# A convolution and mixture-of-experts layer in fp32: low halves of the expert weights made by negated copies and adding DMAs, buffers laid out anew, no float copy of the top indices

## The reference, cut to what matters

```
u  = x @ W_in + b_in; uc = short_conv(u)         # 3 taps, 768 channels
x0, x1, v = split(uc);  v = v * x1
v  = causal_fft_conv(v, filter) + filter_bias    # long convolution over 512 tokens
x  = layernorm(x + (v * x0) @ W_out + b_out)
probs = softmax(x @ gate.T);  top_w, top_idx = top_k(probs, 4)      # 16 experts
y  = sum over the 4 experts of  top_w/sum(top_w) * (silu(x@w1.T) * (x@w3.T)) @ w2.T
x  = layernorm(x + y + shared_expert(x))
```

## Time and profile before

| | |
|---|---|
| three runs | 797.89, 795.56, 797.14 us; median 797.14 |
| profiled execution, first to last instruction (its span) | 696.8 us |
| TensorE | busy 561.5 us (81%), mean granted clock 0.931 |
| VectorE | busy 543.4 us (78%) |
| ScalarE | busy 400.4 us (57%) |
| GpSimd | busy 439.5 us (63%) |
| DMA | 127.69 MB, mean 183 GB/s |

### The profile page before, as it was taken

How to read it: one execution, slowest core, us unless ns; L and a number is a source line. 1 busy time by engine, 2 the same in 40 slices (tenths; PEclk the granted TensorE clock), 3 DMA queues, 4 the chain that set the end, 5 groups by cost and what they waited for, 6 DMA issues and landing times.

```text
span 696.8 us, 13551 instructions
## 1 busy us (share of the span) xinstructions
PE 561.5 (81%) x3356; PEld 491.9 (71%) x3357; DVE 543.4 (78%) x1492; ACT 400.4 (57%) x968; POOL 439.5 (63%) x417
## 2 busy tenths in 40 slices
PE   1789798999999999997268799999899996777600
PEld 0568686888888887876156799899899886767500
DVE  5438699999999999998976566566666568989877
ACT  0635264776767566762134677676677775666632
POOL 2060325486868676767907677777776668777882
PEclk9979899999999999999759999999999999999965
DMA  8339811342333333247843567765655569998674
GB/s 305 108 104 316 287 56 35 107 137 100 115 117 127 105 129 102 97 158 227 263 129 120 185 204 222 233 207 183 187 181 175 166 238 377 279 299 265 239 272 173
DMA packets 77116, 127.69 MB, mean 183 GB/s; under 512 B 10870, under 2 KB 57527, under 8 KB 76474
## 3 DMA queue, kind: packets, MB, share of 16 engines
q1 hardware_dynamic: 45548, 69.34, 32.3%
q0 software_dynamic: 22448, 49.17, 20.1%
q10 hardware_dynamic: 9086, 8.80, 3.7%
HBM read 81.00 MB, written 54.72 MB: 195 GB/s over the span
## 4 chain that ended last, share of the span: by engine, by line
DVE 37%; PE 36%; issue 15%; ACT 4%; POOL 4%; DMA 3%; DVEq 1%; SPq 0%; POOLq 0%; ACTq 0%
PE bank L856 6%; PE bank L857 5%; PE bank L858 5%; PE bank L895 3%; PE bank L687 3%; DVE prodA L1208 2%; POOL token_parts L648 2%; DVE i8f L1265 2%; DVE prodB L1209 2%; PE bank L796 2%; DVE x1c L1129 2%; PE bank L706 2%; PE bank L887 2%; DVE stats L1148 2%; DMA token_parts<-late,wd 2%
## 5 line engine op out<-in xcount | busy, mean ns | idle before, releaser
L648 POOL DMA_INDIRECT token_parts<-late,wd x160 | 156.6, 979 | 67.2 <-issue 40.8
L635 POOL DMA_INDIRECT expert_rows<-row,slot x128 | 131.4, 1026 | 95.5 <-DVE dest L1345 38.8
L856 PE MATMUL bank<-w_hi,xtT_hi 128*128 x320 | 94.0, 294 | 22.2 <-issue 12.6
L1391 DVE TENSOR_TENSOR ta<-bank,tsl 128x128 f32<-128x128 f32 x160 | 46.3, 289 | 66.7 <-ACT tsl L1049 65.0
L1067 ACT ACTIVATE late<-bank,wd 128x256 f32<-128x256 f32 x160 | 76.4, 478 | 37.5 <-DMA token_parts<-late,wd 31.8
L857 PE MATMUL bank<-w_lo,xtT_hi 128*128 x320 | 91.8, 287 | 0.0
L858 PE MATMUL bank<-w_hi,xtT_lo 128*128 x320 | 91.7, 287 | 0.0
L856 PEld LDWEIGHTS bank<-w_hi,xtT_hi 128*128 128x128 f32 x320 | 62.4, 195 | 26.7 <-issue 26.7
L1404 DVE TENSOR_TENSOR xtT_lo<-bank,xtT_hi 128x256 fp32r<-128x256 f32 x160 | 67.6, 423 | 1.1 <-ACT xtT_hi L1060 0.6
L1049 ACT ACTIVATE tsl<-bank 128x128 f32<-128x128 f32 x160 | 44.1, 276 | 39.3 <-PE bank L858 37.5
L1060 ACT CAST xtT_hi<-bank 128x256 fp32r<-128x256 f32 x160 | 61.8, 387 | 6.1 <-PE bank L895 5.7
(11 more groups left out here) (176 smaller groups left out, 1513.5 us busy)
## 6 DMA issues: line engine op xcount, KB each, us to landing
xt<-expert_rows SPq DMA_DIRECT2D x160, 129.0 KB
row<-token_parts SPq DMA_DIRECT2D x12, 640.0 KB, 5.2
more_parts<-token_parts SPq DMA_DIRECT2D x12, 640.0 KB, 8.7
late<-token_parts SPq DMA_DIRECT2D x8, 640.0 KB, 7.8
expert_rows<-in_c_pad SPq DMA_DIRECT2D x2, 2064.0 KB, 14.0
expert_rows<-in_c_pad SPq DMA_DIRECT2D x32, 129.0 KB
xT_hi<-in_xT POOLq DMA_DIRECT2D x8, 512.0 KB, 4.3
xT<-in_xT SPq DMA_DIRECT2D x8, 512.0 KB, 3.9
```

What stands on the lines that cost most here:

```text
L635: pool.indirect_dma_start(out=rows_d, out_offset=bass.IndirectOffsetOnAxis(ap=slot[q][:, n:n + 1], axis=0), in_=row[:, n // TOPK, n % TOPK ...
L648: pool.indirect_dma_start(out=parts_d, out_offset=bass.IndirectOffsetOnAxis(ap=wd[:, v, 1:2].bitcast(U32), axis=0), in_=ty[v % 4], in_offs ...
L856: te_.matmul(ps, x_hi, w_hi, start=first, stop=False)
```

## The change

1. The loads of w2_in and w13 by SP, `low_bits` and `low_bits2` are gone. Instead ACT writes the negated high half into the low half's buffer in body(7) (8192 and 4096 elements on each partition), and POOL adds the weights to it by five DMAs with an adding write: four for w13 after the eighth of the 16 scatters of body(6), one for w2 after the sixteenth. So they come ahead of POOL's bias addition of body(7).
2. PE waits for these five DMAs ahead of the second stage, in place of the subtractions.
3. DVE compares `eidx` with the uint32 indices themselves; `i8f` and one count of `dve_top` go.
4. The buffers are in another order in memory. SP's loads of `xt` wait for the forward transform of batch 7 in place of its inverse.

The diff, without the rest of the new order of buffers (all same sizes; `late` is split in ty_all, s2, ob0 and late_parts, and w2_in is gone):

```diff
-        ARG_N, TOP_N, SLOT_N, TAB_N = 7, 2 * TT + 5, 5, 13
+        ARG_N, TOP_N, SLOT_N, TAB_N = 7, 2 * TT + 4, 5, 13
...
-        def low_bits(eng, ops, n):
-            eng.wait_ge(ld_moe, 32)
-            eng.wait_ge(ld_w13[n], 16)
-            at = slice(n * PART, (n + 1) * PART)
-            ops.tensor_tensor(out=w13_lo[:, at], in0=w13_lo[:, at].bitcast(F32), in1=w13_hi[:, at].bitcast(F32),
-                              op=ALU.subtract).then_inc(lo_made, 1)
...
 # SP, body(7)
-                    sp.wait_ge(dve_conv, 2 * VC * B)
-                    sp.wait_ge(pool_conv, 2 * DC * B)
-                    sp.wait_ge(pe_u, UC * B)
-                    sp.dma_start(w2_in[:, :].rearrange("p (e d) -> p e d", e=E),
-                                 io["w2"].rearrange("e h d -> h e d")).then_inc(ld_w2, 16)
-                    sp.wait_ge(pe_fwd, 2 * NF * B)
-                    sp.wait_ge(dve_Y, 2 * NF * B)
-                    k = E // NPART
-                    for n in range(NPART):
-                        sp.dma_start(w13_lo[:, n * PART:(n + 1) * PART].bitcast(F32)...
 # SP, ahead of the second stage
-            sp.wait_ge(dve_y, DC * B)
+            sp.wait_ge(pe_fwd, 2 * NF * B)
...
 # POOL
-                if isinstance(i, int) and i == B - 1:
-                    for n in range(NPART - 1):
-                        low_bits(pool, nc.gpsimd, n)
...
                         for n in range(TT * TOPK):
+                            if isinstance(i, int) and i == B - 2 and n == TT * TOPK // 2:
+                                low_w13()
                             scatter(n, 1 - q)
+                        if isinstance(i, int) and i == B - 2:
+                            low_w2()
...
+            def low_w13():
+                pool.wait_ge(neg_hi, 1)
+                k = E // NPART
+                for n in range(NPART):
+                    pool.dma_start(w13_lo[:, n * PART:(n + 1) * PART].rearrange("p (e c n) -> p e c n", e=k, c=DC),
+                                   io["w13"][n * k:(n + 1) * k].rearrange("e (c p) n -> p e c n", p=P),
+                                   accum_op=ALU.add).then_inc(ld_w13, 16)
+            def low_w2():
+                pool.wait_ge(neg_hi, 2)
+                pool.dma_start(w2_lo[:, :].rearrange("p (e d) -> p e d", e=E), io["w2"].rearrange("e h d -> h e d"),
+                               accum_op=ALU.add).then_inc(ld_w2, 16)
...
 # PE, ahead of the second stage
-            pe_e.wait_ge(lo_made, NPART + 1)
+            pe_e.wait_ge(ld_w13, 16 * NPART)
+            pe_e.wait_ge(ld_w2, 16)
...
 # ACT, body(7)
+                if is_end(i):
+                    act.wait_ge(ld_moe, 32)
+                    act.wait_ge(dve_conv, 2 * VC * B)
+                    act.wait_ge(pool_conv, 2 * DC * B)
+                    act.wait_ge(pe_u, UC * B)
+                    sc.activation(w13_lo[:, :], w13_hi[:, :].bitcast(F32), ACT.Copy, scale=-1.0).then_inc(neg_hi, 1)
                 if not is0(i):
                     for c in range(DC):
                         act.wait_ge(pe_x1T, 2 * (i - 1) + c + 1)
                         sc.copy(x1T[:, c, :], bank[6 + c][:, :]).then_inc(act_x1T, 1)
+                if is_end(i):
+                    act.wait_ge(dve_Y, 2 * NF * B)
+                    sc.activation(w2_lo[:, :], w2_hi[:, :].bitcast(F32), ACT.Copy, scale=-1.0).then_inc(neg_hi, 1)
...
 # DVE
-                    ve.tensor_copy(i8f[:, :, :], i8[:, :, 0:TOPK]).then_inc(dve_top, 1)
                     ve.reciprocal(rden[:, :], den[:, :]).then_inc(dve_top, 1)
-                    dve.wait_ge(dve_top, n0 + 2 * TT + 2)
-                    ve.tensor_tensor(onehot[:, :, :, :].rearrange("p t k e -> p (t k) e"),
-                                     eidx[:, :].unsqueeze(1).broadcast_to([P, TT * TOPK, E]),
-                                     i8f[:, :, :].rearrange("p t k -> p (t k)").unsqueeze(2).broadcast_to([P, TT * TOPK, E]),
+                    ve.tensor_tensor(onehot[:, :, :, :],
+                                     eidx[:, :].unsqueeze(1).unsqueeze(1).broadcast_to([P, TT, TOPK, E]),
+                                     i8[:, :, 0:TOPK].unsqueeze(3).broadcast_to([P, TT, TOPK, E]),
                                      ALU.is_equal).then_inc(dve_top, 1)
...
-                if isinstance(i, int) and i == B - 1:
-                    low_bits(dve, ve, NPART - 1)
-                    low_bits2()
```

More of the change, by code:

```diff
@@ L175, in build @@
         i8 = sb("i8", [P, TT, 8], U32)
-        i8f = sb("i8f", [P, TT, TOPK])
         den = sb("den", [P, TT])
@@ L229, in build @@
             w_in_lo = ab_("w_in_lo", [P, DC, 3 * D], F32R)
+            xT_hi = ab_("xT_hi", [P, DC, L], F32R)
+            xT = as_read("xT", [P, DC, L])
+            xT_lo = ab_("xT_lo", [P, DC, L], F32R)
             spec = ab_("spec", [P, NF, 2, 2 * D])
@@ L232, in build @@
             V = ab_("V", [P, 2, 2 * D])
+            x1c = ab_("x1c", [P, DC, L])
+            vc = ab_("vc", [P, DC, L])
+            zt = ab_("zt", [P, TT, D])
             prodA = ab_("prodA", [P, 2, 2 * D])
             prodB = ab_("prodB", [P, 2, 2 * D])
-            zt = ab_("zt", [P, TT, D])
-            xT_hi = ab_("xT_hi", [P, DC, L], F32R)
+            x0 = [ab_(f"x0_{q}", [P, DC, L]) for q in range(2)]
             Y = ab_("Y", [P, NF, 2, 2 * D])
-            xT = as_read("xT", [P, DC, L])
@@ L239, in build @@
-            xT_lo = ab_("xT_lo", [P, DC, L], F32R)
-            vc = ab_("vc", [P, DC, L])
             mats = ab_("mats", [P, TT + 2 * NF, L])
             fwd, inv = mats[:, 0:TT, :], mats[:, TT:, :]
-            x0 = [ab_(f"x0_{q}", [P, DC, L]) for q in range(2)]
-            x1c = ab_("x1c", [P, DC, L])
             yx = ab_("yx", [P, DC, L])
-        late = sb("late", [P, (4 + 2 * TT + 2 * PARTS) * D])
-        w2_in = late[:, 0:W2]
-        ty = [late[:, q * D:(q + 1) * D] for q in range(4)]
@@ L252, in build @@
-        s2, ob0 = (late[:, (4 + n * TT) * D:(4 + (n + 1) * TT) * D].rearrange("p (t d) -> p t d", d=D) for n in range(2))
-        ob = [ob0, xtok[:, :, :]]
-        late_parts = late[:, (4 + 2 * TT) * D:]
-        ta = sb("ta", [P, 2, HID])
-        sb("spare", [P, UC * (L + 2) + 2 * DC * 3 * D - (4 + 2 * TT + 2 * PARTS) * D - 2 * HID])
-        w13_lo = sb("w13_lo", [P, W13], F32R)
-        w2_lo = sb("w2_lo", [P, W2], F32R)
-        more_parts = sb("more_parts", [P, TT * TOPK * D])
-        xt = sb("xt", [P, UNROLL, ROW])
+        w13_lo = sb("w13_lo", [P, W13], F32R)
@@ new lines, in build @@
+        sb("spare0", [P, (UC * 2080 + 4 * DC * 3 * D * 2 + 4 * DC * L * 2 - 4 * W13) // 4])
+        w2_lo = sb("w2_lo", [P, W2], F32R)
+        xt = sb("xt", [P, UNROLL, ROW])
+        ta = sb("ta", [P, 2, HID])
+        tsl = sb("tsl", [P, 2, HID])
+        taT_hi = sb("taT_hi", [P, 2, P], F32R)
+        wd = sb("wd", [P, UNROLL, 2])
+        sb("spare1", [P, 2 * DC * L + TT * D - UNROLL * (ROW + 2) - 6 * P])
+        ty_all = sb("ty_all", [P, 4, D])
+        ty = [ty_all[:, q, :] for q in range(4)]
@@ L261, in build @@
         xtT_hi = sb("xtT_hi", [P, 2, DC, P], F32R)
         xtT_lo = sb("xtT_lo", [P, 2, DC, P], F32R)
-        taT_hi = sb("taT_hi", [P, 2, P], F32R)
+        s2 = sb("s2", [P, TT, D])
+        ob0 = sb("ob0", [P, TT, D])
+        ob = [ob0[:, :, :], xtok[:, :, :]]
+        late_parts = sb("late_parts", [P, 2 * PARTS * D])[:, :]
+        more_parts = sb("more_parts", [P, TT * TOPK * D])
         taT_lo = sb("taT_lo", [P, 2, P], F32R)
-        tsl = sb("tsl", [P, 2, HID])
-        wd = sb("wd", [P, UNROLL, 2])
@@ L304, in build @@
             sem(n) for n in ("t_xhi", "t_xlo", "t_wd", "t_sl", "t_a", "t_ahi", "t_alo", "t_yc"))
-        ld_w13 = [sem(f"ld_w13_{n}") for n in range(NPART)]
-        ld_w2, lo_made = sem("ld_w2"), sem("lo_made")
+        ld_w13, ld_w2, neg_hi = sem("ld_w13"), sem("ld_w2"), sem("neg_hi")
         res_out = [sem(f"res_out{q}") for q in range(4)]
```

8 lines of the change are left out of this document (removed).

## The result

| | median | executions |
|---|---|---|
| kernel before | 798.12 us (790.38 to 802.43) | 20 |
| changed kernel | 806.0 us (798.55 to 812.54) | 20 |

Ratio 1.0107, 95% interval 1.0081 to 1.0132: slower by 8 us, where I forecast 11.6 us faster.

The account below looks back on a forecast made before the run. TensorE or VectorE was taken to set the steady pace, and the stalled index copy to hold body(7); -2.7 (index copy) and -8.9 (`residual`) gave -11.6 us, 797.1 to 785.5 us, range 779.5 to 796.

Parts of the forecast that it names:

- Part 2: Body(7): the copy's stall goes, five DMA issues cost 5.5 us ahead of the bias addition, `residual` starts 8.9 us earlier.
- rival B: Part of the gain is lost: adding DMAs at 158 to 110 GB/s, or some 11 us for five issues; 791, chance 0.17.
- Part 1: Bodies 2 to 5: without the index copy the comparison ends earlier; -2.7 us, bounds 0 and -3.1.
- the copy's stall: Body(7): the index copy takes 15.97 us, standing still while POOL adds the bias and makes three low-half parts.
- My rule that one us there is one us of the time: From `residual` of body(7) on, the same instructions follow, so all later work moves by the same 8.9 us.
- Rival D: The one-hot comparison takes over the copy's stall; at most 1.0 us in body(7); chance within the main case's 0.58.
- Part 3: ACT's negated copies for w13 and w2 take 7 and 3.5 us, hidden with 1.9 us of cover: cost 0.
- Part 4: Adding DMAs land at 346.3 (w13, about 22 us) and 357 (w2, 11 us), hidden by 4.7 and 10 us.
- A: Adding DMAs are much slower and the second stage starts late; all gain lost at 110 GB/s, 809.7 at 90; chance 0.15.
- C: PE's clock does not fall during the shorter idle time in body(7): 3.9 us less, 781.6; chance 0.10.
- Part 5: SP's fewer loads ahead of table_row and the new order in memory: nothing gained or lost, 0.

Follow-up runs that it names:

- e8: The changed kernel run once more, on a chip of the 696 us kind, beside the kernel before: 701.22 us, ratio 1.0074.
- e4: The changed kernel with its five DMAs plain instead of adding (output not the reference's): 684.41 us, ratio 0.9843 to the kernel before.
- e13: The changed kernel with w2's adding DMA cut to one expert of sixteen: 691.15 us in one execution, 694.62 for the kernel before.
- e16: The changed kernel with w2's adding DMA in four pieces of 512 KB: 821.62 us against 813.70 before, no ratio given.
- e17: The changed kernel with w2's adding DMA in two pieces of 1024 KB: 820.26 us, ratio 1.0061 to the kernel before.
- e14: The changed kernel with w2's DMA plain, w13's still adding: 688.82 us in one execution, 694.62 for the kernel before.
- e0: The kernel before, unchanged, profiled again in an execution of the timed kind: 801.57 us.
- e3: The kernel before without the float copy of the indices, the comparison reading the uint32 indices: 800.50 us, ratio 1.0025.
- e5: The changed kernel with body(7)'s bias addition moved ahead of w13's adding DMAs: 692.80 us, ratio 0.9974 to the kernel before.
- e6: The changed kernel with bias addition first, w13 adding behind batch 5's last scatter, w2 loaded plain and subtracted on VectorE: 687.52 us, ratio 0.9877.
- e10: e6 with only two parts of w13 adding, the other two loaded plain and subtracted on VectorE: 681.72 us, ratio 0.9802 to the kernel before.
- e11: e5 with all five adding DMAs issued behind batch 5's last scatter: 697.88 us, ratio 1.0027 to the kernel before.
- e15: The changed kernel with w2's adding DMA issued right behind w13's four: 702.02 us in one execution, ratio 1.0107 to the kernel before.
- e12: The changed kernel with w13's adding DMAs behind fourteen of batch 5's scatters instead of eight: 711.17 us in one execution, 694.62 for the kernel before.
- e7: The kernel before with GpSimd's three subtractions moved to VectorE at the end of body(7), index copy kept: 686.50 us, ratio 0.9872.
- e9: e7 without the float copy of the indices: 684.54 us, ratio 0.9853 to the kernel before.

## Why the prediction was wrong, step by step

**Part 2 failed, and with it the sign.** The residual was to start at 339.3; in e8 it starts at 354.82. Two terms make the difference. The five issues cost 6.40 + 2.22 = 8.6 us, not 5.5, and above my bound of 6.3: an adding issue of 1024 KB takes 1.6 us against 0.9 for a plain one of e4. And GpSimd stands for 12.9 us before the fifth. The likely reason is room in its queue: how much w2's DMA asks for decides whether it waits (e13, e16, e17), and an adding DMA of the same bytes waits where a plain one does not (e4, e14). Together that is 16.0 us more than I had, less 0.6 us that the batches before had gained. This is the mechanism that I named under rival B, "the queue takes no more descriptors until it has drained", and argued away by plain loads of 6 MB that went in at once. It was the wrong row: these were plain and nothing stood ahead of them. e4 confirms that plain ones go in, and shows nothing of adding ones. I had priced it with 11 us for the five issues; they took 21.5. With these terms, and Part 1 at the 0.6 us that it gave, the sum for `residual` is -8.9 + 16.0 - 0.6 = +6.5 us, and e8 has +6.6. My rule that one us there is one us of the time held less well: 5.4 us of it are left at tile 1 and 4.9 in the medians.

**Why it is slower, and not just less fast.** Before, GpSimd's bias addition was over 14.4 us ahead of `residual`, since the subtractions stood between: 368.12 and 382.59 in e0, 333.80 and 348.24 in the earlier trace rows. The change puts 6.40 + 12.79 + 2.22 = 21.4 us ahead of the addition. 21.4 less 14.4 less the 0.5 us that the batches before had gained is 6.5, and `residual` is 6.6 us later. The same holds in e8. So the size of the copy's stall, 10.04 us in the timed kind and not 15.97, does not enter the loss.

**Part 1 gained 0.6 us and not 2.7.** On the 696 us kind the comparison takes 1.66 to 2.02 us in bodies 2 to 5 where the copy took 1.9 and it 1.57, so VectorE gained about what I said. TensorE's waits for aT from 125 to 311 us fell from 3.1 to 0.2 us, also as forecast. But the gain did not reach the pace: TensorE now waited 1.6 us at L691 for `slot`, and VectorE 2.7 us at `residual` for TensorE. `residual` of body(6) starts at 302.68 against 303.31. On the timed kind the copy had cost 0.2 us in most bodies, and `residual` waits for TensorE's bank there. Rival D was right in its mechanism: e3 shows it at full size. The one-hot comparison reads two operands from SBUF. The Trainium skill's page SBUF — State Buffer ("SBUF: two separate sides") names just this case, a VectorE instruction with two SBUF inputs against a GpSimd one that reads SBUF, where the later one waits for the whole of the other. The 10.16 us of e3 agree, and go further: GpSimd's three subtractions take 4.5 us each, and the comparison, which came during the first, waited for all three.

**Part 3 was right.** The negations took 7.03 and 3.62 us (7 and 3.5 forecast) and delayed nothing: 2.38 us of waiting for Y stand between them, and in e8 ScalarE is ready for the exponential 3.02 us before VectorE delivers its input.

**Part 4 had the rate right and the landing wrong.** The DMA view of e8 from 326 to 336 (queue: packets, MB, share), where GpSimd's queue moves nearly all:

```profile
DMA packets 2155, 1.91 MB, mean 191 GB/s; under 512 B 288, under 2 KB 2155, under 8 KB 2155
...
q0 software_dynamic: 1899, 1.91, 122.4%
```

191 GB/s is half the plain 390. The Trainium skill's page Collectives: The Full Stack (Part 3, "Why ReduceScatter is half of AllGather") has the same factor for the adding step of a collective. My 22 us for w13 were called the middle of the bounds 10.8 and 27.7, which is 19.3; 22 is the value of half the plain rate. But w13 needs 29.3 us from its first issue (320.6) to its last landing (349.9), not 22: 2.3 us pass before its transfers run and 4 before they reach this rate, and from 336 on SyncE's pad rows move 1.06 MB beside it. The scatters behind it were needed at 351.0 by my sum; e5 has them at 359.18, past my bound of 352. In the changed kernel this costs nothing only because `residual` is later still.

**Rivals.** A (DMAs below 110 GB/s) is refuted by the same rows, although its 809.7 lies near the result. C, the clock, could not come up in the changed kernel, where TensorE idled longer and not less. e4 has the idle time of my forecast and answers it: TensorE stood for 5.75 us, the granted clock fell to 0.50, and the product of aT took 3.78 us as before. Only where the wait was 1.41 us (e5, e6, e10, e11) did it take 1.99. **Part 5**: nothing in the runs speaks for a cost of the layout, since e4 has it too and comes out at 0.9843; the layout alone was not run.

**Open.** How room is counted. w13 and eight scatters take three quarters of w2 and not four (e16). w13, w2 and three scatters fit (e15); w13, two scatters and w2 do not (e12). No simple sum of the requests gives all three, so that it is room is argued and not shown; what is shown is the wait, and what ends it. In e5, e8, e12 and e15 it ended with w13's last landing and not with the earlier ones. Open too is why the second stage took 316 us in e4 to e7, e9 and e11 (from tile 1 to the end of the span), 317.3 in e8, 318.9 in e10 and 320.5 in the first profile.

## What to carry to other kernels

A DMA's issue can block its engine: before a DMA is put ahead of work that others wait for, count what its queue already holds, and put the small urgent instruction first (e5, e6, e10 and e11 do). To take a stall away, move the instruction that holds the resource and not the one that stands at it: e7, which moves three subtractions, is worth 8.8 us, e3, which removes the standing copy, none. And a row of a plain transfer does not price an adding one: here the rate was half, the issue took 1.8 times as long, and the wait for the queue had no counterpart at all.

## What the runs showed of the hardware

- Adding DMAs moved their bytes at 191 GB/s where plain loads ran at 390, and their issue on GpSimd took 6.40 us for four of 1024 KB against 3.63 (e8, e4).
- GpSimd stood 9.85 to 21.55 us ahead of a DMA, until w13's last piece had landed where the traces give that time; the trace shows it as idle time "issue" with no releaser.
- Scatters queued behind 4 MB of adding DMAs landed 36.5 us after the first of these was issued (e5).
- A VectorE comparison of 0.4 us with two inputs in SBUF stood for 10.16 us through three GpSimd subtractions (e3).
- One and the same kernel took 694.6 to 696.4 us on three chips and 798 to 814 on two, with a batch at 36.6 us or at some 43.
